# Sixteen-head window attention on one Trainium2 core: V projected and weighed by itself, instead of joined with the output weights

## The reference, cut to what matters

```python
def attn_layer(x, Wqkv, qs, ksc, Wo):          # Wqkv 128 x 3072, Wo 1024 x 128
    q, k, v = jnp.split(x @ Wqkv, 3, -1)        # 16 heads of 64
    q = l2norm(q) * qs; k = l2norm(k) * ksc
    q = q * cos * scale + rotate_half(q) * sin * scale
    k = k * cos * inv + rotate_half(k) * sin * inv
    out = local_attention(q, k, v)              # windows of 32 queries, 64 keys:
                                                # the window before and its own
    return out.transpose(0, 2, 1, 3).reshape(b, n, INNER) @ Wo
for i in range(DEPTH):                          # 6
    x = attn_layer(shift_tokens(x), Wqkv[i], q_scale[i], k_scale[i], Wo[i]) + x
    x = ffn_layer(shift_tokens(x), ln_g[i], ln_b[i], W1[i], b1[i], W2[i], b2[i]) + x
```

## Time and profile before

| what | us |
|---|---|
| median of 3 runs (lowest, highest) | 4154.56 (4154.02, 4157.87) |
| the profiled execution, its own time | 4155.47 |
| its span, first to last instruction | 4153.7 |
| PE busy | 3814.5 |
| DVE busy | 3258.6 |
| ACT busy | 3109.2 |
| POOL busy | 2498.3 |

### The profile page before, as it was taken

How to read it: one execution, slowest core, us unless ns; L and a number is a source line. 1 busy time by engine, 2 the same in 40 slices (tenths; PEclk the granted TensorE clock), 3 DMA queues, 4 the chain that set the end, 5 groups by cost and what they waited for, 6 DMA issues and landing times.

```text
span 4153.7 us, 101302 instructions
## 1 busy us (share of the span) xinstructions
PE 3814.5 (92%) x30950; PEld 2939.8 (71%) x31328; DVE 3258.6 (78%) x5635; ACT 3109.2 (75%) x7150; POOL 2498.3 (60%) x2247
## 2 busy tenths in 40 slices
PE   6999998899998999988999989999889999899998
PEld 4666665677766777766777667777667776677776
DVE  5877876888867888768888678887688886788876
ACT  4777776788866888857888668887578886688875
POOL 1221221777745777737777457776377774577763
PEclk9999999999998999998999989999989999999999
DMA  2111111000010000010000100000100000000002
GB/s 79 42 32 31 29 39 35 2 0 0 0 28 1 1 0 0 1 28 1 0 0 0 28 1 1 0 0 1 28 1 0 0 0 28 1 1 0 0 1 68
DMA packets 53261, 52.86 MB, mean 13 GB/s; under 512 B 13574, under 2 KB 40452, under 8 KB 51972
## 3 DMA queue, kind: packets, MB, share of 16 engines
q1 hardware_dynamic: 52996, 49.77, 4.5%
HBM read 28.77 MB, written 4.19 MB: 8 GB/s over the span
## 4 chain that ended last, share of the span: by engine, by line
issue 26%; PE 24%; ACT 24%; DVE 21%; ACTq 2%; DVEq 2%; POOL 1%; SPq 0%; DMA 0%; POOLq 0%
PE bank L357 19%; ACT sb_area L668 12%; DVE sb_ssq L1105 10%; DVE sb_smax L1116 6%; ACT sb_area L777 5%; PE bank L416 3%; ACT sb_lnb L786 3%; ACT sb_lnb L789 3%; DVE sb_area L1093 1%; PE bank L503 1%; POOL sb_area L1336 1%; DVE sb_nmx L1013 1%; DVE sb_area L1119 0%; PE bank L532 0%; DVE sb_area L1009 0%
## 5 line engine op out<-in xcount | busy, mean ns | idle before, releaser
L668 ACT ACTIVATE sb_area<-bank 128x512 f32<-128x512 f32 (+4 forms) x3029 | 1570.3, 553 | 259.0 <-PE bank L357 182.3
L357 PE MATMUL bank<-sb_area 128*64 128x64 f32 (+4 forms) x16624 | 1286.1, 274 | 94.9 <-issue 57.8
L1093 DVE TENSOR_TENSOR sb_area<-bank,sb_rots 128x1024 f32<-128x1024 f32 x768 | 939.2, 1224 | 395.2 <-ACT sb_area L777 394.4
L1311 POOL TENSOR_TENSOR sb_area<-sb_area,sb_rn 128x512 f32<-128x512 f32 x768 | 784.8, 1043 | 608.5 <-ACT sb_rn L793 608.5
L1297 POOL TENSOR_TENSOR sb_area<-sb_area 128x512 f32<-128x512 f32 x768 | 967.9, 1278 | 78.3 <-DVE sb_area L1093 76.2
L357 PEld LDWEIGHTS bank<-sb_area 128*64 128x64 f32 (+2 forms) x16624 | 849.5, 151 | 200.6 <-issue 139.1
L357 PE MATMUL bank<-sb_wqk_hi,sb_xwin 128*128 128x512 f32 x1536 | 729.7, 477 | 53.9 <-DVE sb_xwin L1073 43.6
L357 PE MATMUL bank<-sb_area,sb_wvo 128*128 128x256 f32 x3072 | 728.3, 381 | 3.1 <-DVE sb_xT L1151 3.1
L357 PEld LDWEIGHTS bank<-sb_area,sb_wvo 128*128 128x128 f32 x3072 | 555.0, 190 | 78.3 <-issue 12.8
L503 PE MATMUL bank<-sb_ident,sb_area 128*128 128x128 f32 x3072 | 494.9, 285 | 33.4 <-ACT sb_area L668 31.0
L503 PEld LDWEIGHTS bank<-sb_ident,sb_area 128*128 128x128 f32 x3072 | 358.8, 144 | 227.6 <-issue 160.0
(11 more groups left out here) (103 smaller groups left out, 4861.7 us busy)
## 6 DMA issues: line engine op xcount, KB each, us to landing
sb_xwin<-sb_p SPq DMA_DIRECT2D x256, 64.0 KB, 2.0
sb_area<-in_Wqkv SPq DMA_DIRECT2D x7, 1024.0 KB, 5.8
sb_area<-in_WvT SPq DMA_DIRECT2D x7, 512.0 KB, 7.3
sb_wo_bd<-in_Wo SPq DMA_DIRECT2D x14, 256.0 KB, 8.2
sb_area<-in_x SPq DMA_DIRECT2D x4, 512.0 KB, 5.7
sb_area<-in_x SPq DMA_DIRECT2D x8, 256.0 KB, 2.9
x_plus_causal<-sb_area SPq DMA_DIRECT2D x8, 256.0 KB, 2.3
out<-sb_area SPq DMA_DIRECT2D x8, 256.0 KB, 3.5
```

The costliest lines, as they stand in the source:

```text
L357: return nc.tensor.matmul(o, a, b, start=start, stop=stop, skip_group_check=True)
L668: return nc.scalar.activation(o, i, ACT.Copy)
L1093: tt_(t12[:, c % 2, :, :].rearrange("p u (h d) -> p u h d", h=8), src, bc(rots[:, tt, s, :, :], [P, 2, 8, D], 2), ALU.mult).then_inc(S["ro ...
L1311: pt_(qn[:, c, :].rearrange("p (h d) -> p h d", h=8), qsum[:, c % 2, :].rearrange("p (h d) -> p h d", h=8), r, ALU.mult).then_inc(S["qn"], 1)
```

## The change

V becomes a projection of its own. `project_values` (lag 2, once a half) projects 512 columns of V by three products into the bank that `turn_p` uses (`tbank`), and ACT copies them to `vt` (two tiles deep). A tile's rows are also wanted 32 tokens earlier, for the windows that begin half-way: two DMAs a tile on SP's queue move `vt` by 32 rows into `vsh` (96 rows and 32 rows of 4 KB). P's transpose is copied to `pbd` in two copies of 64 rows with zeros between, laid out so that one product weighs both of a half's two key groups of a head: stationary is the 128 x 64 of a head's values, moving 64 columns, the result 64 rows of a bank, two heads above one another. That makes 16 products a half (32 passes) instead of 4 (8 passes), one ACT copy of the results instead of two, and `project_out` takes two heads at once: half as many products. `join_weights`, `windows` and their ACT copies go. All 3072 columns of Wqkv are now split, six chunks instead of four. `turn_p` waits until ACT has copied the values out of the bank, `project_values` until it has copied P, and the values' copy waits for the moves of the tile before and for the weighing that last read its buffer.

Core of the diff:

```diff
-                        for part_ in range(2):
-                            cols = slice(256 * part_, 256 * part_ + 256)
-                            for w2_ in range(2):
-                                keys = slice(64 * w2_, 64 * w2_ + 64)
-                                m = mm(ybank[w2_][:, cols], xw[keys, tt, wp, :], pT[keys, wp, cols])
-                                if part_:
-                                    m.then_inc(S["yy"], 1)
+                        values = vt[:, tt % 2, :] if wp else vsh[:, tt % 2, :]
+                        for hp in range(HP):
+                            for h2 in range(2):
+                                h = 2 * hp + h2
+                                m = mm(ybank[wp][64 * h2:64 * h2 + 64, hp * 64:(hp + 1) * 64], values[:, h * D:(h + 1) * D],
+                                       pbd[:, wp, hp // 2, 2 * (hp % 2) + h2, :, :].rearrange("p a b -> p (a b)"))
+                        m.then_inc(S["yy"], 1)
...
-                            for h in range(4 * k, 4 * k + 4):
-                                m = mm(mbank[:, 0:256], wvo[:, h, :], ysb[:, hf, :, h * WIN:(h + 1) * WIN],
-                                       h == 0, h == HEADS - 1)
+                            for hp in range(2 * k, 2 * k + 2):
+                                m = mm(mbank[:, 0:256], wo[:, hp, :], ysb[:, hf, :, hp, :], hp == 0, hp == HP - 1)
...
                         turn_p(wp)
                         project(2 * wp + 1)
                         score(wp)
-                        if wp == 0:
-                            windows()
                         weigh(4 - wp, 1 - wp)
                         turn_qk(2 * wp + 1)
+                        project_values(wp)
                         project_out(wp)
-                    join_weights()
...
+                    def project_values(wp):
+                        if not (v := behind(t, i, part, 2)):
+                            return
+                        tt, bt = v
+                        if part == 0 and t == 2:
+                            pe.wait_ge(S["w_split"], 12 * l + 2 * (4 + wp) + 2)
+                            pe.wait_ge(S["vev"], g_of(bt) * 8 + wp)
+                        pe.wait_ge(S["ptev"], g_of(i) * 8 + (2 * (t - 3) + wp + 1 if t >= 3 else 0))
+                        w = slice(2 * INNER + wp * 512, 2 * INNER + (wp + 1) * 512)
+                        split3(tbank[:, :], xs_hi[:, tt, :], xs_lo[:, tt, :], wqkv_hi[:, w], wqkv_lo[:, w])\
+                            .then_inc(S["vproj"], 1)
...
-                        copy(pT[:, wp, :], tbank[:, :]).then_inc(S["ptev"], 1)
+                        act.wait_ge(S["yy"], m_ + 1)
+                        src = tbank[:, :].rearrange("p (j h q) -> p j h q", j=4, h=4)
+                        for w2_ in range(2):
+                            r = slice(64 * w2_, 64 * w2_ + 64)
+                            m = copy(pbd[r, wp, :, :, w2_, :], src[r])
+                        m.then_inc(S["ptev"], 1)
...
+                        act.wait_ge(S["vproj"], g * 2 + wp + 1)
+                        if not (part == 0 and t == 2):
+                            act.wait_ge(S[f"vshift{(tt + 1) % 2}"], 32 * (2 * g_of(bt) + (tt - 1) // 2 + 1))
+                            act.wait_ge(S["yy"], g * 2)
+                        copy(vt[:, tt % 2, wp * 512:(wp + 1) * 512], tbank[:, :]).then_inc(S["vev"], 1)
...
                         exp(wp)
+                        projected_values(wp)
                         norms(wp)
...
+                for g in range(l * B * TT, (l + 1) * B * TT):
+                    tt = g % TT
+                    sp.wait_ge(S["vev"], g * 2 + 2)
+                    if g:
+                        sp.wait_ge(S["yy"], g * 2)
+                    sp.dma_start(vsh[32:128, tt % 2, :], vt[0:96, tt % 2, :]).then_inc(S[f"vshift{tt % 2}"], 16)
+                    sp.dma_start(vsh[0:32, tt % 2, :], vt[96:128, (tt - 1) % 2 if tt else 0, :]).then_inc(S[f"vshift{tt % 2}"], 16)
```

More of the change, by code:

```diff
@@ L36 @@
 MASKED = -1.0e30
-AREA = 25856
+AREA = 27392
 OUT_PARTS = (((6, 3), (5, 1)), ((5, 2), (4, 0)))
@@ L155, in build @@
         xn_all = take(NTOK)
-        wqk_raw, wv_raw = take(2 * INNER), take(HP, C)
+        wqkv_raw = take(3 * INNER)
         w1, w2 = take(2 * FF), take(3, C)
@@ L529, in turn_p @@
                         pe.wait_ge(S["pn"], m_ + 2)
-                        pe.wait_ge(S["ptev"], m_)
+                        values = 2 * (t - 2) + wp
+                        pe.wait_ge(S["vev"], g_of(i) * 8 + (min(values, 4 * TT) if part == 2 else values))
+                        if part == 2 and t == 2 * TT + 2:
+                            pe.wait_ge(S["ptev"], m_)
                         for j in range(4):
@@ L739, in heads_of_weights @@
             def heads_of_weights(l):
-                act.wait_ge(S["w_loaded"], (l + 1) * (5 * 16))
-                for c in range(4):
+                act.wait_ge(S["w_loaded"], (l + 1) * (3 * 16))
+                for c in range(6):
                     w = slice(c * 512, (c + 1) * 512)
-                    copy(wqk_hi[:, w], wqk_raw[:, w]).then_inc(S["w_split_h"], 1)
+                    copy(wqkv_hi[:, w], wqkv_raw[:, w]).then_inc(S["w_split_h"], 1)
             heads_of_weights(0)
@@ L747, in _, with heads_of_tokens @@
             with act.Fori(0, layers) as l:
-                def heads_of_tokens(tt, bt):
+                def heads_of_tokens(tt, bt, again=False):
                     g = (l * B + bt) * 4 + tt
+                    if again:
+                        act.wait_ge(S["vproj"], g * 2 - 6)
                     act.wait_ge(S["xs_part"], g + 1)
@@ L761, in g_of @@
                         return l * B + bt
-                    def joined_weights():
-                        if part or t >= 4:
-                            return
-                        act.wait_ge(S["wvo_mm"], 4 * l + t + 1)
-                        copy(wvo[:, 4 * t:4 * t + 4, :], mbank[:, :].rearrange("p (a b) -> p a b", a=4))\
-                            .then_inc(S["wvo_ready"], 1)
                     def square(c):
@@ L827, in turned_p, with projected_values @@
                         act.wait_ge(S["pt"], m_ + 3)
-                        act.wait_ge(S["yy"], m_ * 2)
-                        copy(pT[:, wp, :], tbank[:, :]).then_inc(S["ptev"], 1)
+                        act.wait_ge(S["yy"], m_ + 1)
[4 more added lines that the diff above has]
+                        m.then_inc(S["ptev"], 1)
+                    def projected_values(wp):
+                        if not (v := behind(t, i, part, 2)):
+                            return
+                        tt, bt = v
+                        g = g_of(bt) * 4 + tt
+                        act.wait_ge(S["vproj"], g * 2 + wp + 1)
[3 more added lines that the diff above has]
+                        copy(vt[:, tt % 2, wp * 512:(wp + 1) * 512], tbank[:, :]).then_inc(S["vev"], 1)
                     def weighed(lag, wp):
@@ L835, in weighed @@
                         m_ = g_of(bt) * 8 + 2 * tt + wp
-                        act.wait_ge(S["yy"], m_ * 2 + 3)
+                        act.wait_ge(S["yy"], m_ + 3)
                         act.wait_ge(S["oo"], g_of(bt) * 2 + tt // 2)
-                        copy(ysb[:, tt // 2, 4 * (tt % 2) + wp, :], ybank[0][:, :]).then_inc(S["yev0"], 1)
-                        act.wait_ge(S["yy"], m_ * 2 + 4)
-                        copy(ysb[:, tt // 2, 4 * (tt % 2) + wp + 2, :], ybank[1][:, :]).then_inc(S["yev1"], 1)
-                    def windows():
-                        if not (v := behind(t, i, part, 1)):
-                            return
-                        tt, bt = v
-                        g = g_of(bt) * 4 + tt
-                        act.wait_ge(S["xwt"], g + 1)
-                        if not (part == 0 and t - 1 < TT):
-                            act.wait_ge(S["yy"], g * 4 - 10)
-                        copy(xw[:, tt, :, :], rbank[:, 0:256].rearrange("p (w c) -> p w c", w=2)).then_inc(S["xwev"], 1)
+                        copy(ysb[:, tt // 2, 2 * (tt % 2):2 * (tt % 2) + 2, :, wp * WIN:(wp + 1) * WIN].rearrange("p w h q -> p h w q"),
+                             ybank[wp][:, :].rearrange("p (h w q) -> p h w q", h=HP, w=2)).then_inc(S["yev"], 1)
                     for wp in range(2):
@@ L856, in step @@
                         square(2 * wp + 1)
-                        if wp == 0:
-                            windows()
-                            if not (part == 0 and t == 0) and (v := behind(t, i, part, -1)):
-                                heads_of_tokens(*v)
+                        if wp == 0 and not (part == 0 and t == 0) and (v := behind(t, i, part, -1)):
+                            heads_of_tokens(*v, not (part == 0 and t < TT - 1))
                         weighed(4 - wp, 1 - wp)
```

101 lines of the change are left out of this document (35 added, 66 removed).

## The result

The changed kernel took 4362.34 us (median of 4 runs, 4360.68 to 4362.61); the kernel before took 4156.22 us beside it (4 runs, 4154.02 to 4158.47). The ratio is 1.0495 with an interval of [1.0477, 1.0513]: slower, by 206 us. 4373 us had been forecast. The profiled execution took 4362.61 us, its span 4360.7 us, at a mean granted clock of 0.970 against 0.971 before.

What follows compares the result with a forecast made beforehand. The prediction took a circle of ACT and DVE, without PE, as the bound. 41.8 - 2.1 - 3.6 - 1.2 = 34.9 us a layer, x 6 = 209, + 10 = +219 us, gave 4373 us; range 4280 to 4460 us.

Steps and rivals of the forecast that it cites:

- a circle of ACT and DVE without PE: Mid-layer attention: ACT's norms, squares and copies, then DVE's work until the next norms, set halves of 7.40 and 6.79 us.
- Copies of P, +1.44 us a step: Between ACT's two squares: a 64-row pair for a single copy adds 0.71 and 0.73 us, +41.8 us a layer.
- ACT's run behind the second square, nothing: ACT from second square to next norms: the added values copy just fits before DVE lets the norms start, cost nothing.
- rival 2: ACT's run after the second square outgrows DVE's, values' copy 0.2 us late: +70 us, 4443 us, chance 0.13.
- PE, nothing: PE's products in each half: about 6.8 us needed against 8.1 and 7.5 us available, so no cost.
- DMA, nothing: Two moves of V a tile on SP's queue end at 4 to 6.5 us, before the next values copy: no cost.
- Weights, +10 us: Head of a layer: two more DVE subtractions for six weight chunks, +1.43 us, seven times, +10.0 us.
- Joins, drain and last update, -6.9 us a layer: Per layer: dropped ACT join copies -2.1 us, less PE work in the drain -3.6 us, last token update -1.2 us.
- 1, overlapping copies: ACT's 64-row copies of P overlap, the second adding only 0.50 us: 77 us less, 4296 us, chance 0.13.
- 3, PE as the pace: PE sets the step's pace, so its saved work makes the kernel faster: 3992 us, chance 0.05.
- 4, late moves of V: Both moves land after 8.5 us, holding ACT's first values copy about 1 us a step: +190 us, 4563 us, chance 0.05.
- 5, the clock: PE's idle time drops its clock to a mean of 0.75: +450 us, 4823 us, chance 0.04.

Runs made afterwards that it cites:

- experiment 1: Kernel before with only P's transpose copied as two copies of 64 rows instead of one of 128: 4413.44 us, ratio 1.0626.
- experiment 4: ACT's copies of P moved behind the second square: 4135.76 us in the kernel before (ratio 0.9953), 4039.98 us in the changed kernel (ratio 0.972).
- experiment 7: Changed kernel with V projected by one product instead of three: 4369.29 us, ratio 1.0512.
- experiment 8: Changed kernel with ACT's copy of the projected V cut to 8 columns: 4358.59 us; with that copy made twice: 4515.35 us.
- experiment 2: Changed kernel with P copied in one 128-row copy, the split into two key groups left out: 4110.09 us, ratio 0.9893.
- experiment 5: Changed kernel with the low parts of V's two weight chunks computed after the next layer's first tiles are loaded: 4354.84 us, ratio 1.0479.

## Why the prediction was right

*The bound.* It was taken from the chain and the waits against the busy shares: a circle of ACT and DVE without PE. Experiments 1, 4, 7 and 8 each bear on it. A copy of P inside the circle costs its full length, behind the second square a part of it, and 0.46 us less of PE's products a half changes no step. But in the kernel before the circle led PE by less than 0.1 us a step (experiment 4). The forecast could leave PE out because the change made the circle longer and PE's work shorter; a change that shortens the circle needed the other bound too.

*Copies of P, +1.44 us a step.* The halves grew by 0.74 us (8.14 against 7.40) and 0.62 us (7.40 against 6.78); 0.71 and 0.73 had been said. The pair itself is worth 1.45 us by experiment 2 and 1.48 us by experiment 1. The missing 0.1 us of the second half is another gain, which the prediction didn't have: from the norms to the first square it was 0.92 us before (2596.95 to 2597.87) and is 0.82 us now (2663.64 to 2664.46), with the copy of P in one piece too. 6 x 29 x 0.1 = 17 us. Its cause is open: in experiment 1 the second half still had 0.92 us. The forecast was 11 us too high; that it came so near is partly luck, for without the two small costs below that it did not have (4 us ahead of the first layer, and what PE's waits for the moves cost) it would have been a few us further off.

*ACT's run behind the second square, nothing.* Right, with little to spare: 0.04 us in the first half (experiment 8). A few tenths more would have been rival 2.

*PE, nothing.* Right: 6.8 us a half had been said; from `project` to `project` it was 7.28 and 8.36 us with 0.39 and 1.47 us of waits before `turn_p`, 6.89 us each. The three products of V take 0.78 us up to the output's first (0.31, 0.23 and 0.24 us from start to start), between the 0.70 us taken and the 0.90 us set as the most.

*DMA, nothing.* Right in the full pipeline (the page's part 6: KB each, median us to landing):

```profile
sb_area<-sb_area SPq DMA_DIRECT2D x192, 384.0 KB, 3.5
sb_area<-sb_area SPq DMA_DIRECT2D x192, 128.0 KB, 3.4
```

They were issued 0.57 us apart, and both had landed 3.9 to 5.7 us after the first was issued, where 4 to 6.5 us had been estimated. That is in time for the next values copy, 7.7 us after the issue (2655.37 to 2663.11). In each layer's drain it was not quite nothing: there PE waited for the moves before its last products with shifted values, 0.8 to 0.9 us a layer:

```profile
PE bank L361 <- DMA sb_area<-sb_area: 5.1, 6, 0.9
```

The prediction had looked at the deadline of ACT's copy alone. At most 5 us of the time are this wait; how much of it counts no run shows.

*Weights, +10 us.* 7.5 to 8.5 us (experiment 5). *Joins, drain and last update, -6.9 us a layer.* Not measured one by one. The stretch from first to last norms grew by 37.1 us, where 29 steps of 1.36 us alone make 39.4, so about 2.3 us are left for the joins (2.1 said). The stretch between the layers gave 3.1 us; with the 1.2 us that the weights added there, drain and last update gave 4.3 us (3.6 + 1.2 said).

*The rivals.* 1, overlapping copies: excluded by experiment 1, 0.60 us each. The Trainium skill's rule ("ScalarE: Activation LUTs", section "What ACT_TABLE_LOAD costs") gave 0.52 us for the extra copy and 4304 us. The page gives its figures for tiles of 128 partitions, and the 128-row copies here come near them (0.48 to 0.49 us apart). The 64-row copies do not, and the measurement decides. 2: excluded by experiment 8. 3, PE as the pace: excluded by experiment 7; yet it holds for the kernel before once P is moved (experiment 4), and with P moved the whole change is worth 96 us (4135.8 - 4040.0). 4, late moves of V: none in the full pipeline; in the drain PE waited 5.1 us for them in all. 5, the clock: 0.970 against 0.971, with waits of 0.4 and 1.5 us in turn; in experiment 7, with 0.46 us less work a half, the drops began. So the change stood nearer to this rival than "on the safe side" said. The Trainium skill ("TensorE: Matmul & The Clock Gate", section "A second HAM failure mode: psum-queue depth-cycling") tells of frequent small idles between groups of products that make the clock swing. The changed kernel's trace does not bear that out, for its clock from 2620 to 3060 us is 1.00 beside such waits; experiment 7's trace, with longer waits, agrees with it.

## What to carry to other kernels

Before pricing a saving on the busiest engine, find the circle of waits that closes from one step to the same point of the next, and ask which instructions lie in it: here 117 us less PE work was worth nothing and one copy made in two pieces cost 250 us. The same copies a few places later, in a stretch where their engine waits anyway, cost much less, until that engine had no idle time left there; only then did the change's savings count. Look also at how far the next bound is: here it was less than 0.1 us a step away. And look at the drain by itself: waits for the moves of V that the full pipeline never showed stood in the drain of every layer. Where a copy can be split either way, the split by columns was the cheap one here.
